# A decoder layer on one core: sums into y by accumulating DMA, a product on GpSimd, and a reordered start

## The reference

```
x = x + attention(layernorm(x))          # 32 query heads, 8 key heads, head width 64, rotary, causal
x = x + ssm(ctx, z=layernorm(x))         # ctx: 4 x 256 x 128; 256 channels, 16 states
x = x + ffn(layernorm(x))                # 704 wide, integer weights with scales, silu gate
```

```
state_n = state_n * exp(delta * A_n) + delta * u * B_n      # n = 0..15, a scan over t
y = sum over n of state_n * C_n  +  D * u ;   result = y * silu(z)
```

## Time and profile before

| | |
|---|---|
| median of 3 runs | 469.43 us (469.29 to 469.91) |
| the profiled execution | 470.13 us |
| its span, first to last instruction | 468.3 us |
| PE busy | 390.7 us, 83% |
| DVE busy | 380.0 us, 81% |
| ACT busy | 266.4 us, 57% |
| POOL busy | 231.9 us, 50% |
| mean granted TensorE clock | 0.962 of full speed |

### The profile page before, as it was taken

How to read it: one execution, slowest core, us unless ns; L and a number is a source line. 1 busy time by engine, 2 the same in 40 slices (tenths; PEclk the granted TensorE clock), 3 DMA queues, 4 the chain that set the end, 5 groups by cost and what they waited for, 6 DMA issues and landing times.

```text
span 468.3 us, 7732 instructions
## 1 busy us (share of the span) xinstructions
PE 390.7 (83%) x2605; PEld 311.4 (66%) x2636; DVE 380.0 (81%) x479; ACT 266.4 (57%) x775; POOL 231.9 (50%) x260
## 2 busy tenths in 40 slices
PE   4648998887999599967998699958988569899997
PEld 2434776766778477755776587746867448688885
DVE  1666567889998999899989998997899998666532
ACT  1435789766866467636764576555635456833221
POOL 2362252367657565846664577556375458311000
PEclk9979999999999989998999799979999889999999
DMA  9636546352433034333142331430314311000000
GB/s 224 119 77 122 122 87 203 126 162 52 131 102 78 18 106 139 94 118 114 36 123 46 113 114 46 136 112 24 113 29 129 98 39 25 0 2 24 22 24 22
DMA packets 50615, 40.64 MB, mean 87 GB/s; under 512 B 32296, under 2 KB 42736, under 8 KB 50576
## 3 DMA queue, kind: packets, MB, share of 16 engines
q1 hardware_dynamic: 38560, 32.64, 24.5%
q0 software_dynamic: 5120, 5.25, 5.0%
q10 hardware_dynamic: 6896, 2.25, 2.2%
HBM read 26.36 MB, written 1.18 MB: 59 GB/s over the span
## 4 chain that ended last, share of the span: by engine, by line
PE 32%; DVE 27%; issue 23%; POOL 10%; ACTq 2%; ACT 2%; DMA 2%; SPq 1%; DVEq 0%; POOLq 0%
DVE nmax L724 7%; DVE state L802 7%; PE ps_so L1077 5%; PE ps_p L1290 5%; PE ps_p L1064 5%; DVE state L809 5%; PE ps_so L1273 5%; POOL rc L413 4%; PE ps_p L1175 3%; PE ps_r L1129 3%; POOL y L419 2%; POOL qt L269 2%; PE ps_so L1157 2%; POOL kt L280 2%; ACTq L255 1%
## 5 line engine op out<-in xcount | busy, mean ns | idle before, releaser
L490 ACT ACTIVATE prob<-ps_so,nmax 128x256 f32<-128x256 f32 (+1 forms) x256 | 104.7, 445 | 72.6 <-DVE nmax L724 72.6
L419 POOL TENSOR_TENSOR y<-y,state 128x1024 f32<-128x1024 f32 x32 | 82.9, 2589 | 60.8 <-DVE state L815 60.6
L413 POOL TENSOR_TENSOR rc<-rc,rs 128x512 f32<-128x512 f32 x40 | 56.6, 1414 | 100.8 <-DVE rs L712 62.0
L809 DVE TENSOR_TENSOR_SCAN state<-decay,state 128x1024 f32<-128x1024 f32 x32 | 95.1, 2971 | 1.1
L1064 PE MATMUL ps_p<-xt_all,wq 128*128 128x256 f32 x256 | 65.7, 400 | 10.6 <-DVE rs L716 5.8
L724 DVE TENSOR_REDUCE nmax<-ps_so 128x2 f32<-128x512 f32 (+1 forms) x96 | 60.3, 683 | 15.8 <-PE ps_so L1088 15.8
L1157 PE MATMUL ps_so<-pt,vv 128*64 128x256 f32 x256 | 45.5, 433 | 29.9 <-ACT pt L496 29.9
L269 POOL DMA_DIRECT2D qt<-rc x128 | 63.5, 502 | 12.2 <-POOL rc L413 9.1
L496 ACT ACTIVATE pt<-ps_r 128x512 f32<-128x512 f32 x96 | 53.4, 590 | 27.7 <-PE ps_r L1129 22.7
L1175 PE MATMUL ps_p<-wo,attn_t 128*128 128x256 f32 x256 | 61.2, 386 | 8.3 <-DVE x L832 8.3
L1064 PEld LDWEIGHTS ps_p<-xt_all,wq 128*128 128x128 f32 x256 | 47.6, 196 | 24.3 <-DVE rs L716 7.8
(11 more groups left out here) (107 smaller groups left out, 518.0 us busy)
## 6 DMA issues: line engine op xcount, KB each, us to landing
bc<-bc_scratch SPq DMA_DIRECT2D x32, 512.0 KB, 4.6
qt<-rc SPq DMA_DIRECT2D x128, 32.0 KB, 2.0
qt<-rc POOLq DMA_DIRECT2D x128, 32.0 KB, 1.8
kt<-kt SPq DMA_DIRECT2D x8, 256.0 KB, 3.0
wo<-wo_t SPq DMA_DIRECT2D x1, 2048.0 KB, 9.5
wq<-wqkv_t SPq DMA_DIRECT2D x24, 64.0 KB, 3.1
kt<-rc SPq DMA_DIRECT2D x32, 32.0 KB, 2.0
kt<-rc POOLq DMA_DIRECT2D x32, 32.0 KB, 1.7
```

What stands on the lines that cost most here:

```text
L413: nc.gpsimd.tensor_tensor(rc[:, r % 2, :, :], rc[:, r % 2, :, :], rs[:], ALU.add).then_inc(rope_add, 1)
L419: nc.gpsimd.tensor_tensor(y[:, v % 2, :], y[:, v % 2, :], state[:, v % 2, :], ALU.add).then_inc(state_free, 1)
L490: nc.scalar.activation(o, i, ACT.Exp, bias=nmax[:, r, c:c + 1], accum_out=rsum[:, r, GRP + head:GRP + head + 1]).then_inc(exp_done, 1)
L809: nc.vector.tensor_tensor_scan(state[:, v % 2, :], decay[:, v % 2, :], state[:, v % 2, :], 0.0, ALU.mult, ALU.add).then_inc(decay_free, 1)
```

## The change

- `add_y` is no longer a POOL instruction but a DMA with addition, state into y, issued by POOL and counted on `y_sum[v % 2]`. It waits for `hc_done(v)` and for the landing of the DMA before it in the same half.
- `drive` of a unit's first scan is a POOL instruction, placed at the head of the unit behind `add_y` of the last unit's first scan and ahead of `add_rope`; it waits for B, for the landing of y's DMA v-2 and for `times_c(v-2)`. A second scan's `drive` stays on DVE and waits for the landing of v-2.
- In the start: q weights 2 and 4 are loaded by SP, 3 by ACT behind the taps, 5 to 7 in units 0 to 2. k's first head goes by two DMAs on SP and two on POOL to both halves of the partitions, and unit 0's scores wait for these and no longer for `double_k(0)`, which copies the other three heads. DVE does one convolution step, then k's and q's rope, then the other five, and the layer-norm of batches 1 to 3 behind the maxima of unit 0. PE and ACT are ordered to match.
- The store of B and C moves to unit 1 of SP and their first load to unit 2; ACT's wait for the store moves to the first decay.

```diff
 # POOL
-                pool.wait_ge(state_free, v + 1)
-                nc.gpsimd.tensor_tensor(y[:, v % 2, :], y[:, v % 2, :], state[:, v % 2, :], ALU.add
-                                        ).then_inc(state_free, 1)
+                if v >= 2:
+                    pool.wait_ge(y_sum[v % 2], 16 * (v // 2))
+                nc.gpsimd.dma_start(y[:, v % 2, :], state[:, v % 2, :], accum_op=ALU.add).then_inc(y_sum[v % 2], 16)
+
+            def drive(v):
+
+                n = v // 2
+                pool.wait_ge(ssm_ready, 5)
+                pool.wait_ge(bc_in[n % 2], (n // 2 + 1) * 32)
+                if v >= 2:
+                    pool.wait_ge(y_sum[v % 2], 16 * (v // 2))
+                    pool.wait_ge(hc_done, v - 1)
+                nc.gpsimd.tensor_tensor(state[:, v % 2, :], du[:, v % 2, :], bc[:, n % 2, 0, :], ALU.mult
+                                        ).then_inc(drive_done, 1)
 
             add_rope(("k", 0))
-            move_k(nc.gpsimd, 0, range(KG // 2, KG), k_pool)
+            move_first_k(nc.gpsimd, 1)
             add_rope(("q", 0))
             move_q(nc.gpsimd, 0, range(GRP // 2, GRP), q_pool)
-            ln_rstds(1, B, 2)
+            move_k(nc.gpsimd, 0, range(KG // 2, KG), k_pool)
             add_rope(("q", 1))
             move_q(nc.gpsimd, 1, range(GRP // 2, GRP), q_pool)
+            ln_rstds(1, B, 2)
...
             for u in range(UNITS):
                 for v in scans(u - 1)[:1] if u else ():
                     add_y(v)
+                for v in scans(u)[:1]:
+                    drive(v)
                 if u + 2 < UNITS:
                     add_rope(("q", u + 2))
 # SP
-            move_k(sp, 0, range(KG // 2), k_sp)
+            load_wq(sp, 2)
+            move_first_k(sp, 0)
             move_q(sp, 0, range(GRP // 2), q_sp)
+            move_k(sp, 0, range(1, KG // 2), k_sp)
+            load_wq(sp, 4)
             double_k(0)
 # ACT
-            load_wq(nc.scalar, 2)
-            load_wq(nc.scalar, 3)
...
+            copy_xt(0)
             first_tap(0)
-            copy_xt(0)
...
             first_tap(1)
+            load_wq(nc.scalar, 3)
...
-            act.wait_ge(bc_out, 16)
 # DVE
-            convolve(0)
+            convolve(0, (1,))
             dve.wait_ge(tab_sb, 4)
             rope(("k", 0))
             rope(("q", 0))
-            convolve(1)
+            convolve(0, range(2, DC))
+            convolve(1, range(1, DC))
+            rope(("q", 1))
+            negmax(0)
             dve.wait_ge(x_in[1], 16)
             ln_stats(1, B)
-            rope(("q", 1))
-            negmax(0)
             ln_apply(1, B, 2)
...
                 for v in todo[:1]:
-                    drive(v)
                     scan(v)
...
-            dve.wait_ge(state_free, UNITS + 2)
+            for e in range(EB):
+                dve.wait_ge(y_sum[e], 16 * NS)
 # PE
-            project_ctx(0)
+            project_ctx(0, (0,))
             transpose_x(0)
+            project_ctx(0, (1,))
...
-            project_ctx(1)
             fill(("k", 0))
             fill(("q", 0))
+            project_ctx(1, range(2))
```

More of the change, by code:

```diff
@@ L90, in scans @@
     return range(at, at + SCANS[u])
+SECOND = [v for u in range(UNITS) for v in scans(u)[1:]]
 def decoder_layer(nc, x, ctx_t, wqkv_t, wo_t, cos_t, sin_t, inproj_t, ssm_par, xproj_t, dtproj_t,
@@ L197, in decoder_layer @@
         k_pool = [sem(f"k_pool{r}") for r in range(2)]
+        k_first = [sem("k_first_sp"), sem("k_first_pool")]
         k_in = [sem(f"k_in{r}") for r in range(2)]
@@ L232, in decoder_layer @@
         decay_free = sem("decay_free")
-        drive_done = sem("drive_done")
+        drive_done, drive_own = sem("drive_done"), sem("drive_own")
         hc_done = sem("hc_done")
-        state_free = sem("state_free")
+        y_sum = [sem(f"y_sum{e}") for e in range(EB)]
         x1_done = sem("x1_done")
@@ L270, in move_q, with move_first_k, k_sp_due @@
                                     ).then_inc(landed[u % 2], 16)
+        def move_first_k(queue, c):
+            queue.wait_ge(rope_add, 1)
+            for to in (0, HD):
+                queue.dma_start(kt[to + c * HALF:to + (c + 1) * HALF, 0, 0, :], rc[0:HALF, 0, c, :]
+                                ).then_inc(k_first[c], 16)
+        def k_sp_due(j):
+            return 16 * (k_moves * (j // 2 + 1) - (2 if j % 2 == 0 else 0))
         def move_k(queue, j, heads, landed):
@@ L305, in double_k @@
             def double_k(j):
-                sp.wait_ge(k_sp[j % 2], 16 * k_moves * (j // 2 + 1))
+                sp.wait_ge(k_sp[j % 2], k_sp_due(j))
                 sp.wait_ge(k_pool[j % 2], 16 * k_moves * (j // 2 + 1))
-                sp.dma_start(kt[HD:P, j % 2, :, :], kt[0:HD, j % 2, :, :]).then_inc(k_in[j % 2], 16)
+                i = 0 if j else 1
+                sp.dma_start(kt[HD:P, j % 2, i:, :], kt[0:HD, j % 2, i:, :]).then_inc(k_in[j % 2], 16)
             def load_bc(n):
@@ L346, in _ @@
                 load_wk(1)
[L347 to L353, removed]
             for u in range(UNITS):
@@ L358, in _ @@
                     double_k(u // KG + 1)
-                if u < 2:
-                    load_wq(sp, 6 + u)
+                if u < 3:
+                    load_wq(sp, 5 + u)
+                if u == 1:
+                    sp.wait_ge(xdbl_sb, 2)
+                    sp.dma_start(bc_scratch, xdbl[DR:XR, :]).then_inc(bc_out, 16)
+                if u == 2:
+                    sp.wait_ge(bc_out, 16)
+                    load_bc(0)
                 if u == 2:
@@ L516, in decays @@
                     act.wait_ge(ssm_ready, 5)
+                    act.wait_ge(bc_out, 16)
                 act.wait_ge(decay_free, v + 1)
@@ L705, in rope @@
                     else:
-                        dve.wait_ge(k_sp[i % 2], 16 * k_moves * (i // 2 + 1))
+                        if i == 0:
+                            dve.wait_ge(k_first[0], 16 * 2)
+                            dve.wait_ge(k_first[1], 16 * 2)
+                        dve.wait_ge(k_sp[i % 2], k_sp_due(i))
                         dve.wait_ge(k_pool[i % 2], 16 * k_moves * (i // 2 + 1))
@@ L733, in reciprocals, with convolve @@
                 nc.vector.reciprocal(rinv[:, u % 2, :], rsum[:, u % 2, :]).then_inc(rinv_done, 1)
-            def convolve(e):
+            def convolve(e, lags):
                 dve.wait_ge(tap_done, e + 1)
@@ L740, in convolve @@
                 src = ps_so[:, 2 * e:2 * e + 2, :].rearrange("p h (b s) -> p (h b) s", b=B // 2)
-                for lag in range(1, DC):
+                for lag in lags:
                     if lag > 1:
@@ L800, in drive @@
                 dve.wait_ge(bc_in[n % 2], (n // 2 + 1) * 32)
-                dve.wait_ge(state_free, v + 1)
+                dve.wait_ge(y_sum[v % 2], 16 * (v // 2))
                 nc.vector.tensor_tensor(state[:, v % 2, :], du[:, v % 2, :], bc[:, n % 2, 0, :], ALU.mult
-                                        ).then_inc(drive_done, 1)
+                                        ).then_inc(drive_own, 1)
             def scan(v):
-                dve.wait_ge(drive_done, v + 1)
+                if v in SECOND:
+                    dve.wait_ge(drive_own, SECOND.index(v) + 1)
+                else:
+                    dve.wait_ge(drive_done, v + 1 - sum(w < v for w in SECOND))
                 dve.wait_ge(decay_done, v + 1)
@@ L1016, in transpose_x, with project_ctx @@
                 last.then_inc(xt_ps, 1)
-            def project_ctx(e):
+            def project_ctx(e, halves):
                 pe.wait_ge(ctx_in, 32)
-                for h in range(2):
+                for h in halves:
                     nc.tensor.matmul(ps_so[:, 2 * e + h, :], inproj[:, e * P:(e + 1) * P],
@@ L1071, in scores @@
                 pe.wait_ge(q_pool[r], 16 * q_moves * (u // 2 + 1))
-                pe.wait_ge(k_in[j % 2], 16 * (j // 2 + 1))
+                if u == 0:
+                    pe.wait_ge(k_first[0], 16 * 2)
+                    pe.wait_ge(k_first[1], 16 * 2)
+                else:
+                    pe.wait_ge(k_in[j % 2], 16 * (j // 2 + 1))
                 def dot(bank, col, h, t, keys, start=False):
```

1 line of the change is left out of this document (removed).

## The result

The changed kernel takes 482.66 us (median of 4 runs, 477.17 to 484.97) beside 469.36 us for the kernel before in the same session: ratio 1.0242, 95% interval 1.0152 to 1.0332. The kernel is slower beyond the noise; whether by more than 2% the interval leaves open. One of the four runs, 484.97, was a slow one; the median holds it, the ratio and its interval don't. The forecast was 454 us with a range of 436 to 476. The execution profiled here took 477.17 us, its span is 475.4 us, 7.1 over the span of before; it is the fastest of the four, so the trace shows about half of the median's loss of 13.3.

The account below looks back on a forecast made before the run. The loop was taken as DVE's, PE close behind. Start -7.0, single-scan units -2.4, groups -5.4, units 25 to 28 -2.0, end +1.4 sum to -15.4; 470.13-15.4-0.7 = 454 us, range 436 to 476.

Parts of the forecast that it names:

- The start: Before unit 1: reordered weight DMAs and k moves let unit 0's scores start at 23.1 instead of 30.26; -7.0 us.
- they have until unit 5: Start: B and C's store and load can move to units 1 and 2 without cost; units 1 to 4 forecast 0.
- The excluded instructions: Loop: two-input SBUF instructions of DVE and POOL exclude each other; 22 us over 32 scans, 9 over 32 products.
- single-scan units: Units with one scan: scan starts 4.85 us after the head against 4.83, nothing won; with units 5, 7, 8 -2.4 us.
- The DMA's prices: y's accumulating DMA: issue 1.0 us on POOL, landing 5.8 us from start of issue, 7.5 in company.
- rival (c): POOL's issue of y's DMA costs 2.0 us, some 20 units lose 0.8 each: 471 us; chance 0.15.
- rival (a): y's DMA lands in 4.4 us, so four groups give -16 us: 440 us; chance 0.25.
- 7.5 beside bc's pair of loads or another such DMA: y's accumulating DMA in company: lands 7.5 us after start of issue, instead of 5.8.
- The groups: Units with two scans and the one behind, four groups: -1.35 us each, -5.4 in all.
- Nearly all is given back: Two-scan groups: scan 7 gains 4.8 us, but scan 8 starts at 174.8 against 175.25.
- (b): Units behind two-scan units: slower landing, 8 us alone and 9.7 in company, becomes the bound: 483 us; chance 0.18.
- turning point of 9.3 us: Landing in company from about which the slower-landing rival decides, the groups eating what the start gives.

Follow-up runs that it names:

- Experiment 7: First load of B and C moved from unit 2 to unit 3: changed kernel 475.57 us, accum_dve 442.35, new start with the old loop 462.44.
- accum_dve: Changed kernel with every product du*B on DVE again, the accumulating DMA kept: 448.39 us, ratio 0.9567.
- no_bc: Changed kernel without the loads of B and C from the third pair of scans on (first two pairs reused): 455.01 us, ratio 0.9675.

## Why the prediction was wrong

**The start** was right: -7.3 against -7.0. k's rope begins at 12.52 (12.8 was forecast), unit 0's scores at 22.98 (23.1), the first maxima at 26.28 against 33.56. One price inside it was off both ways: SP's first eight weight DMAs take 8.58 us, 1.07 each and not 0.8, and the four new ones 2.09, so SP is free of them at 17.1, near the 16.9 of the forecast because two misses cancel. That what follows is free, "they have until unit 5", was the first wrong step: it looked at who needs B and C and not at what SP issues right behind them. wo and q's moves for unit 5 met them, +4.2 us in units 1 to 4 of the trace. Experiment 7 shows it.

**The excluded instructions** were read rightly and are most of what the loop's change had to win: "Over 32 scans this is 32*(2.97-2.29) = 22 us", and the DMA alone takes 21.8 off the scans and 20 off the time. But the forecast never asked what each half is worth alone. That nothing comes of the product in single-scan units was right: units 5 to 9 take 50.0 us with it on POOL and with it on DVE (accum_dve). Behind two-scan units it costs 20 us, since there POOL waits in front of the product, and q's addition and moves stand behind it.

**The DMA's prices.** Issue 1.0: measured 0.95, right, and so rival (c) is out. Landing alone 5.8: measured 4.6, better than assumed and near rival (a)'s 4.4. **The step that failed is the next, "7.5 beside bc's pair of loads or another such DMA".** In unit 12 the two sums take 8.3 and 10.0; in the five places where two sums and both loads meet, the later sum takes 9.8 to 11.0 us. The company was counted as one other transfer or pair; here it is three, 2 MB within 1.4 us. And the forecast let only y's landing count, while POOL's product waits for B and C too, and a load that the sums delay in their turn may come last (9.4 us for that of 161.3). With no sum over 7.2 us and no late load (no_bc) the kernel takes 455.0.

**The groups.** Up to scan 7 the working holds. By the clock of before (the changed kernel runs 3.6 us ahead at unit 9) the sum that product 7 waits for lands after 6.0 us (5.8 was forecast) and scan 7 ends at 163.9 (163.6). Then product 8 ends at 176.7 instead of 173.5. Of these 3.2 us the late sum accounts for 1.3 (it lands at 172.4, forecast 171.1) and the load of B and C, later still, for the other 1.9. Scan 8 ends at 180.1 instead of 177.1. For the time past that the forecast says "Nearly all is given back" and adds a small win; in truth q's moves behind the product come late, PE waits 6.7 us in unit 12 and comes back at half its clock. Forecast -1.35 a group, measured +2.6.

**The rivals.** (b) comes nearest to what happened. Its place is right (POOL's product at the head of the units behind two-scan units, rope's addition and four moves queued behind, PE's q two units on), and landings in company lie on both sides of its turning point of 9.3 us. Its landing of 8 us alone was not met (4.6), and it has no part for late loads of B and C. That its 483 is next to 482.7 is luck: it adds 13.6 to the kernel before, the trace has +7.1. (b) had no loss in unit 4, +12 over the groups (measured +10.4), +6 in units 25 to 28 (measured -2.3). What spoke for (b) was in the rows: in company the 512 KB of B and C already took 4.6 us, and the sums add 16 MB (32 times 512 KB) to the same engines. Against it stood only that a single sum has a whole unit of time, which is true and says nothing of the second. The chance of 0.18 and the range's end at 476 were too low for a price that no row bounded. Rival (a)'s landing of 4.4 was nearly right for a sum alone, and its 440 is far off, since behind two-scan units the sums are not alone.

## What to carry to other kernels

Before an engine's work is moved to the head of another engine's list, list what it will wait for and what it will hold: here a sum and two loads in the company of another sum, and behind them an addition, eight moves and PE's scores. Test the halves of such a change apart: one was worth -20 us and the other +11, and +34 on top of the first. Mending one wait at such a head is not enough either, the next one takes its place: with the sums issued earlier the product still cost 25 us. Issue first what is needed first, over all queues: here the long sum ahead of moves that are needed later was worth 6 to 14 us, and a 3 MB block of loads right before the small moves that the next unit needs cost 5 to 7.

## What the runs showed of the hardware that was not expected

- A 128x1024 fp32 accumulation inside SBUF takes 0.95 us of POOL's time to issue and lands 4.6 us after the start of issue when alone; a plain copy takes 0.57 and 2.9. In the company of two 512 KB loads and a second sum the earlier sum takes 6.2 to 8.6 us and the later 9.8 to 11.0 (five places).
- The prediction counted on rope's addition to hold the scan off, and the traces show how: in unit 12 POOL's addition starts at 173.12, the scan that the product released at 173.18, and the scan stands for the rest of the addition (3.35 us against 2.29 alone). The Trainium skill ("SBUF — State Buffer", SBUF: two separate sides) says that whoever starts first keeps the shared pair for the whole instruction; the trace agrees here. In the kernel before the scan of 163.84 took 4.59 us although POOL's sum starts 0.07 us after it; at that distance the starts in the trace don't tell who has the pair.
- A late move costs more than its lateness: after waits of 6.72 us (unit 12) and 3.88 us (unit 15) PE came back at 1.2 GHz (granted clock 0.50 from 178 to 182 and from 218 to 222), and the scores took 2.93 us instead of 1.58.
